# A scan as four plus three accumulating matmuls a batch: four consecutive rows on a partition, and the steps of neighbouring batches interleaved

## What is computed

```python
def _L0_xattn_ref(q, k, v):
    kv = jnp.swapaxes(k * v, 0, 1)
    def step(r, kv_t):
        r = DECAY * r + kv_t          # DECAY = 0.9
        return (r, r)
    _, rs = jax.lax.scan(step, r0, kv)
    return q * jnp.swapaxes(rs, 0, 1)
...
x = x + _L0_xattn_ref(_layernorm(x), ctx, ctx)
x = x + _L0_ffn_ref(_layernorm(x), w1, b1, w2, b2)
```

## Time and profile before

| | |
|---|---|
| median of 3 runs | 1266.23 us (1264.81 to 1266.30) |
| the profiled execution's own time | 1265.31 us |
| its span, first to last instruction | 1263.5 us |
| scan stage, by the chain that ended last | 0 to 315.9 us |
| scales and first quantization | 315.9 to 329.2 us |
| first product (second stage) | 329.2 to 800.5 us |
| second product (third stage) | 807 to 1263.5 us |
| busy: PE, ACT, DVE, POOL | 96%, 78%, 69%, 13% of the span |
| mean granted clock of PE | 0.987 of full |

### The profile page before, as it was taken

How to read it: one execution, slowest core, us unless ns; L and a number is a source line. 1 busy time by engine, 2 the same in 40 slices (tenths; PEclk the granted TensorE clock), 3 DMA queues, 4 the chain that set the end, 5 groups by cost and what they waited for, 6 DMA issues and landing times.

```text
span 1263.5 us, 15533 instructions
## 1 busy us (share of the span) xinstructions
PE 1213.5 (96%) x5386; PEld 562.1 (44%) x5386; DVE 872.2 (69%) x1262; ACT 979.9 (78%) x1211; POOL 162.3 (13%) x394
## 2 busy tenths in 40 slices
PE   5998999999699999999999999799999999999997
PEld 2444444444344444444444444344444444444443
DVE  4887999886577777777777777566545655654554
ACT  4788999887577777777777776688887888888776
POOL 2646556444000000000000000000000000000000
PEclk9999999999799999999999999899999999999999
DMA  9999999972277799999999998699999999999998
GB/s 354 403 406 333 389 363 341 346 277 81 118 321 289 305 394 407 359 365 362 362 358 351 348 363 317 229 334 419 418 417 417 417 418 417 417 418 416 416 417 325
DMA packets 134614, 448.78 MB, mean 355 GB/s; under 512 B 10740, under 2 KB 10760, under 8 KB 123400
## 3 DMA queue, kind: packets, MB, share of 16 engines
q1 hardware_dynamic: 94744, 331.40, 66.2%
q10 hardware_dynamic: 39792, 116.40, 25.8%
HBM read 254.81 MB, written 192.94 MB: 354 GB/s over the span
## 4 chain that ended last, share of the span: by engine, by line
PE 80%; POOL 6%; issue 5%; DVE 4%; DMA 3%; ACT 2%; SPq 1%; ACTq 0%; POOLq 0%; DVEq 0%
PE ps L833 35%; PE ps L875 33%; PE ps L811 9%; PE ps L855 2%; DMA xq<-hidden_scratch 2%; POOL xq L444 2%; DVE st L644 1%; DVE st L630 1%; DVE xq L639 1%; DMA xq<-in_x_dram 1%; POOL rstd L436 1%; POOL cs_bc L428 1%; ACT xq L478 1%; ACT xq L589 0%; SPq L317 0%
## 5 line engine op out<-in xcount | busy, mean ns | idle before, releaser
L875 PE MATMUL ps<-w2T,xq 128*128 128x512 f16 x2048 | 446.4, 381 | 4.2 <-ACT xq L589 3.8
L833 PE MATMUL ps<-xq,w1T 128*128 128x512 f16 x2048 | 448.7, 380 | 1.4 <-DVE xq L710 1.4
L589 ACT ACTIVATE xq<-xq,hb,hs 128x512 f16<-128x512 f32 x494 | 357.3, 801 | 83.6 <-PE ps L875 57.5
L701 DVE TENSOR_REDUCE work<-xq 128x2 f32<-128x1024 f32 x255 | 311.0, 1220 | 125.9 <-ACT xq L534 125.9
L534 ACT ACTIVATE xq<-ps 128x1024 f32<-128x1024 f32 x255 | 260.9, 1023 | 123.1 <-PE ps L833 122.9
L875 PEld LDWEIGHTS ps<-w2T,xq 128*128 128x128 f16 x2048 | 200.0, 98 | 250.6 <-ACT xq L589 9.8
L811 PE MATMUL ps<-xq,work 128*128 128x512 f32 x640 | 283.0, 603 | 24.7 <-ACT xq L468 24.7
L833 PEld LDWEIGHTS ps<-xq,w1T 128*128 128x128 f16 x2048 | 199.1, 98 | 237.0 <-issue 1.9
L749 DVE TENSOR_TENSOR work<-ps,cs_bc 128x512 f32<-128x512 f32 x128 | 88.4, 691 | 185.0 <-PE ps L875 178.6
L811 PEld LDWEIGHTS ps<-xq,work 128*128 128x128 f32 x640 | 122.9, 193 | 178.0 <-issue 161.0
L478 ACT ACTIVATE xq<-ps,ones,cs_bc 128x512 f32<-128x512 f32 x128 | 98.9, 772 | 24.8 <-PE ps L811 23.8
(11 more groups left out here) (99 smaller groups left out, 444.9 us busy)
## 6 DMA issues: line engine op xcount, KB each, us to landing
hidden_scratch<-xq SPq DMA_DIRECT2D x240, 512.0 KB, 6.0
xq<-hidden_scratch SPq DMA_DIRECT2D x232, 512.0 KB, 21.2
work<-x_scratch ACTq DMA_DIRECT2D x42, 1024.0 KB, 11.4
xq<-in_ctx_dram ACTq DMA_DIRECT2D x31, 1024.0 KB, 9.2
xq<-in_x_dram SPq DMA_DIRECT2D x24, 1024.0 KB, 12.0
x_scratch<-xq SPq DMA_DIRECT2D x24, 1024.0 KB, 8.4
out_dram<-work ACTq DMA_DIRECT2D x24, 1024.0 KB, 12.0
xq<-in_L_ffn_w_dram SPq DMA_DIRECT2D x8, 1024.0 KB, 7.8
```

The costliest lines, as they stand in the source:

```text
L589: act.activation(hq[c % HQ], src[:, c % 2, :], ACT.Relu, bias=hb[:, q:q + 1], scale=hs[:, q:q + 1]).then_inc(h_scaled, 1)
L701: dve.tensor_reduce(hmax[:, b * NF + 2 * q:b * NF + 2 * q + 2], src, AX.X, ALU.max).then_inc(kept_maxed, 1)
L833: last = pe.matmul(bank, w1T[:, k, f * P:(f + 1) * P], xq_rows(b, k), start=(k == 0), stop=(k == KD - 1))
L875: last = pe.matmul(acc_bank(s, i), src[:, i * P:(i + 1) * P], w2T[:, q, :], start=first, stop=final)
```

## The change

**Four consecutive rows a partition.** Row `4 p + i` of a batch now lies on partition `p` as tile `i`, for x, ctx and the output; a partition's part of a transfer is one piece of 8 KB.

**Seven matmuls.** With that order the scan over a batch is a scan over partitions of the sum of a partition's four rows (each weighted), and then a step from row to row within the partition. A batch has one bank. `scan_first(j, k)` for `k` = 0..3 sums four products into it, and what stands there is tile 0. `scan_next(j, i)` for `i` = 1..3 adds one product with a scaled identity (`own_mat`) to the same bank, and what stands there is tile `i` up to a factor that is put into the constants of the statistics (`half_x`, `per_row_x`, `eps_x`). ACT has to have read tile `i - 1` from the bank before `scan_next(j, i)` may write: a wait of PE for ACT (`scan_scaled`) in each of the three steps, and ACT waits for PE (`scan_ready`) for the next one.

**Interleaving.** To have work between these steps, PE's list puts the four of batch j+2 between the single steps of batches j and j+1. Tiles are worked off in the order (j+1, 0), (j, 2), (j+1, 1), (j, 3), written out in `tiles`, and `scans` is the order in which banks come ready. ACT, DVE and the stores of SP count by these lists.

**Around it.** `ctx` has four buffers and not three, x is loaded six batches ahead and not five, x's statistics are taken four batches ahead and not three (`XLEAD`), the statistics rings hold eight batches and not four, `g1` has four tiles in turn and not two batches, POOL's list has the statistics of both kinds in odd batches and the rounding in even ones, and the square of batch j+3 stands at the end of ACT's batch j, before the steps for the weights. The load of the first weight quarter stands after five x batches and not after three. POOL and DVE make some more constants at the start. The second and third stage are unchanged but for the output's row order.

```diff
-    x_rows = x.rearrange("b (i p) d -> b p i d", p=P)
-    ctx_rows = ctx_in.rearrange("b (i p) d -> b p i d", p=P)
-    out_rows = out.rearrange("b (i p) d -> b p i d", p=P)
+    x_rows = x.rearrange("b (p i) d -> b p i d", p=P)
+    ctx_rows = ctx_in.rearrange("b (p i) d -> b p i d", p=P)
+    out_rows = out.rearrange("b (p i) d -> b p i d", p=P)
...
-CS = 3
-RING = 4
-LEAD = 5
+CS = 4
+RING = 8
+XLEAD = 4
+LEAD = 6
...
+    scans, tiles = [(0, 0)], []
+    for j in range(-1, NB):
+        scans += [t for t in ((j + 1, 1), (j, 3), (j + 1, 2), (j + 2, 0)) if 0 <= t[0] < NB]
+        tiles += [t for t in ((j + 1, 0), (j, 2), (j + 1, 1), (j, 3)) if 0 <= t[0] < NB]
+    scan_at = {t: n for n, t in enumerate(scans)}
+    tile_at = {t: n for n, t in enumerate(tiles)}
...
             def load_ctx(j):
-                wait_count(act, scan_ready, (j - CS + 1) * NI)
+                if j >= CS:
+                    act.wait_ge(scan_ready, scan_at[(j - CS, NI - 1)] + 1)
...
-                act.wait_ge(scan_ready, u + 1)
-                wait_count(act, x2_done, u + 1 - 2 * NI)
-                act.activation(g1[j % 2][:, i, :], scan_bank(j, i), ACT.Identity, bias=ones[:, 0:1],
+                act.wait_ge(scan_ready, scan_at[(j, i)] + 1)
+                wait_count(act, x2_done, n + 1 - len(g1))
+                act.activation(g1[n % len(g1)], scan_bank(j), ACT.Identity, bias=ones[:, 0:1],
...
             square(0)
+            factors(0, 0)
+            square(1)
+            factors(0, 1)
+            square(2)
             for j in range(NB):
-                factors(j, 0)
-                factors(j, 1)
                 if j + 1 < NB:
-                    square(j + 1)
+                    factors(j + 1, 0)
                 factors(j, 2)
-                factors(j, 3)
+                if j + 1 < NB:
+                    factors(j + 1, 1)
                 if j + CS < NB:
                     load_ctx(j + CS)
+                factors(j, 3)
+                if j + 3 < NB:
+                    square(j + 3)
                 for m in weights_at(j - 1):
                     int_weights(m)
                 for m in weights_at(j - 3):
...
+            for n in range(2, NU):
+                j, i = divmod(n - 2, NI)
+                product(n)
+                y_stats(n - 1)
+                if j < NB - 1:
+                    x_stats(j + XLEAD, i)
+                if i == NI - 1:
+                    for m in weights_at(j):
+                        weight_scales(m)
...
-            def scan(j, i):
-                u = j * NI + i
-                wait_count(pe, scan_scaled, u - 5)
-                kv, bank = ct[j % CS], scan_bank(j, i)
-                terms = [(k, kv[:, i - k, :]) for k in range(i + 1)]
-                for k, rows in terms:
-                    last = pe.matmul(bank, decay_mat[:, k * P:(k + 1) * P], rows, start=(k == 0), stop=(k == terms[-1][0]))
-                last.then_inc(scan_ready, 1)
+            def scan_first(j, k):
+                if not 0 <= j < NB:
+                    return
+                if k == 0:
+                    pe.wait_ge(ctx_squared, j + 1)
+                    if j >= 6:
+                        pe.wait_ge(scan_scaled, tile_at[(j - 6, NI - 1)] + 1)
+                last = pe.matmul(scan_bank(j), decay_mat[:, k * P:(k + 1) * P], ct[j % CS][:, k, :], start=(k == 0), stop=(k == NI - 1))
+                if k == NI - 1:
+                    last.then_inc(scan_ready, 1)
+
+            def scan_next(j, i):
+                if not 0 <= j < NB:
+                    return
+                pe.wait_ge(scan_scaled, tile_at[(j, i - 1)] + 1)
+                pe.matmul(scan_bank(j), own_mat[:, (i - 1) * P:i * P], ct[j % CS][:, i, :], start=False, stop=True, skip_group_check=True).then_inc(scan_ready, 1)
...
-            for j in range(NB):
-                pe.wait_ge(ctx_squared, j + 1)
-                for i in range(NI):
-                    scan(j, i)
+            for j in range(-1, NB):
+                scan_first(j + 2, 0)
+                scan_next(j + 1, 1)
+                scan_first(j + 2, 1)
+                scan_next(j, 3)
+                scan_first(j + 2, 2)
+                scan_next(j + 1, 2)
+                scan_first(j + 2, 3)
                 for m in weights_at(j - 2):
                     turn_weights(m)
```

More of the change, by code:

```diff
@@ L387, in _ @@
             gp.memset(ones[:, :], 1.0)
-            gp.memset(decays, DECAY)
+            gp.memset(decays, DECAY ** NI)
+            for i in range(NI):
+                gp.memset(half_x.rearrange("p (n i) -> p n i", i=NI)[:, :, i], 0.5 * DECAY ** -i)
+                gp.memset(per_row_x.rearrange("p (n i) -> p n i", i=NI)[:, :, i], DECAY ** (-2 * i) / D)
+                gp.memset(eps_x.rearrange("p (n i) -> p n i", i=NI)[:, :, i], LN_EPS * DECAY ** (-2 * i))
             gp.memset(neg_half[:, :], -0.5)
@@ L393, in _ @@
             gp.wait_ge(gp_step, 1)
-            for m, w in ((impulse, 4 * P), (ident[:, :], P), (ident_b[:, :], P)):
+            for i in range(NI):
+                part = impulse[:, i * P:(i + 1) * P]
+                gp.affine_select(out=part, in_=part, compare_op=ALU.not_equal, fill=DECAY ** (NI - i) if i else 1.0, base=1 if i else 0,
+                                 pattern=[[-1, P]], channel_multiplier=1)
+            for i in range(1, NI):
+                gp.memset(decays[:, i * P:i * P + 1], 0.0)
+            for m in (ident[:, :], ident_b[:, :]):
                 last = gp.affine_select(out=m, in_=m, compare_op=ALU.not_equal, fill=1.0, base=0,
-                                        pattern=[[-1, w]], channel_multiplier=1)
+                                        pattern=[[-1, P]], channel_multiplier=1)
             last.then_inc(consts_ready, 1)
@@ L405, in step, with row_stats @@
                 gp.wait_ge(gp_step, stepped[0])
-            def row_stats(pw, st, mean, factor):
+            def row_stats(pw, st, mean, factor, per, halves, floor):
                 n = st.shape[1]
@@ L415, in row_stats @@
                 gp.tensor_tensor(mean, t[0], factor[:, 0:n], ALU.mult)
[L416 to L418 removed]
+                gp.tensor_tensor(t[3], t[1], per[:, 0:n], ALU.mult)
+                step(gp.tensor_tensor(t[4], t[2], halves[:, 0:n], ALU.mult))
+                gp.tensor_tensor(t[5], t[3], floor[:, 0:n], ALU.add)
                 step(gp.tensor_tensor(t[6], t[4], t[4], ALU.mult))
@@ L448, in _ @@
             x_stats(x_group[1])
-            for j in range(NB):
-                if j % 2 == 1 and j + 1 < NB:
-                    x_stats(x_group[j + 1])
-                if j % 2 == 0 and j >= 2:
-                    y_stats(y_group[j - 1])
+            x_stats(x_group[2])
+            for j in range(NB - 2):
+                if j % 2 == 1:
+                    if j + XLEAD < NB:
+                        x_stats(x_group[j + XLEAD])
+                    y_stats(y_group[j])
                 for m in weights_at(j):
@@ L611, in _ @@
             link(dve.tensor_tensor_scan(decay_mat, decays, impulse, 0.0, ALU.mult, ALU.add))
+            for i in range(1, NI):
+                link(dve.tensor_scalar(own_mat[:, (i - 1) * P:i * P], ident[:, :], DECAY ** -i, None, ALU.mult))
             def weight_scales(m):
```

68 lines of the change are left out of this document (37 added, 31 removed).

## The result

The changed kernel took 1271.88 us (median of 8 runs, 1270.03 to 1275.49), the kernel before beside it 1265.05 us (8 runs, 1264.57 to 1266.40). The ratio is 1.0056, 95% interval 1.0043 to 1.0069. The forecast of 1251 us was wrong, in sign and in range. The profiled execution took 1270.98 us, its span is 1269.2 us, mean granted clock 0.969 (0.987 before).

What follows compares the result with a forecast made beforehand. The scan stage's end was taken to carry the kernel's end, PE alone bounding the last 13 batches. Last bank read 304.4 us for 315.9, -11.5, and third stage -2 gave -13.5: 1251 us, range 1225 to 1266.

Steps and rivals of the forecast that it cites:

- the third stage: Output stores in longer pieces need less DMA time, so late PE and ACT waits go: -2 us (bounds 0 and -6).
- the handshake: Scan stage: ACT and PE wait for each other over the later tiles, about 0.55 us a batch, bounds 0 and 1.2.
- the count of falls: Scan stage: the clock falls seven times, once in each later pair of batches with weights.
- start, to square(3): Scan stage's start, both lists walked through from ACT's first centring at 18.6 us: square(3) at 35.5 us.
- seven pairs with weights: Scan stage: pairs of batches with weight quarters, each 20.5 us including a fall of the clock, 143.5 us together.
- last copies, iterations 18 to 27: Scan stage: last weight copies 1.8 us, then ten iterations without weights at 7.6 us, 76 us.
- The clock: Scan stage: PE idles some 4.2 us behind weight steps, seven times; the clock then falls and the bank comes 1.85 us later.
- Transfers: 8 KB pieces run at 417 GB/s, not 387: a batch's DMA floor is 7.5 us instead of 8.1.
- the second regime: Scan batches without weights, PE alone bounding at 8.6 us; only there are the saved matmuls (2.6 us a batch) on the path.
- The fifth: Rival, slower: the clock falls in iterations without weights too, twelve falls at 1.8 us, 1273 us; chance 0.10.
- The second (no fall): Rival: the clock stays up in the scan stage's pairs with weights, 12.5 us less, 1239 us; chance 0.23.
- The third (engines at their floors): Rival: handshake, transfers and POOL are not felt, ACT's own work bounds the scan stage, 1219 us; chance 0.12.

Runs made afterwards that it cites:

- e6: Kernel before with only the new row order for x, ctx and output (scan then runs over wrongly ordered rows): 1266.92 us, ratio 1.0012.
- e5: Changed kernel with only the output's transfers back in 2 KB pieces (output rows in another order): 1268.71 us, ratio 1.0032 to the kernel before.
- e12: As e11, but each output store cut into two transfers of every second tile, 2 KB pieces, row order kept: 1239.64 us.
- e10: Changed kernel with three useless matmuls more a batch, so ten again in the new order: 1305.11 us, ratio 1.0311 to the kernel before.
- e2: Changed kernel plus two or four useless matmuls in each of nine PE gaps behind ACT's weight steps: 1254.45 us, ratio 0.9915 to the kernel before.
- e11: As e4, plus one useless matmul in each of two PE gaps in iterations with weights: 1242.88 us, ratio 0.9828 to the kernel before.
- e3: Changed kernel with ACT's weight steps spread one by one between the tiles of the next iterations: 1247.55 us, ratio 0.9868 to the kernel before.
- e4: Changed kernel with weight steps spread between tiles and the ctx load behind the fourth tile's bank read: 1238.84 us, ratio 0.9802.
- e9: Changed kernel with weight steps spread, ctx load between fourth tile's centring and read, two useless matmuls in iterations with weights: 1237.86 us.
- e1: Changed kernel with ACT's ctx load moved behind the fourth tile's bank read: 1263.52 us, ratio 0.9986 to the kernel before.
- e7: Changed kernel with ACT's ctx load moved between the fourth tile's centring and its bank read: 1265.11 us, ratio 0.9994 to the kernel before.

## Why the prediction was wrong, step by step

The sum had 304.4 us for the last bank read's end; it is 316.7, 12.3 us more. The total was to be -13.5 us and the span grew by 5.7. No single step carries that; nearly all erred to one side. The steps that failed are the third stage (-2 us, where it lost 3.4), the handshake (0.55 us a batch, where it took 0.86) and the count of falls (seven, where nine came).

| step | predicted | measured | off |
|---|---|---|---|
| start, to square(3) | 35.5 | 37.7 | +2.2 |
| iteration 1 and first pair | 25.6 | 25.6 | 0.0 |
| seven pairs with weights | 143.5 | 147.9 | +4.4 |
| last copies, iterations 18 to 27 | 77.8 | 83.9 | +6.1 |
| end of the stage | 22 | 21.5 | -0.5 |
| last read to first product | 0 (to 1) | +1.0 | +1.0 |
| second stage | 0 | +0.4 | +0.4 |
| third stage | -2 | +3.4 | +5.4 |

**The start.** ACT's first centring began at 19.20 and not at 18.6 us, ACT stood 0.90 us for PE before the read at 30.41, and 0.76 us before the centring at 34.50, the handshake's price below: together the 2.2 us.

**The clock: right in kind.** All seven idle times that I named (3.87 us; I had 4.2) were followed by a fall, on average at the predicted price: 21.13 a pair, the mean of 20.7 to 22.1, is 2 x 7.78 + 3.72 + 1.85. The Trainium skill ("TensorE: Matmul & The Clock Gate", Part 1) has the throttled state as the default, by which all seven fall; the trace of the changed kernel agrees, nine of nine from 1.98 us on. **The count failed**: the fall belongs to the iteration behind the weight step, so the seventh of 3.87 us falls behind the last pair, and the last copies alone (1.98 us idle) give another. Both landed in what I had called iterations without weights: some 4.3 of the 6.1 us.

**The handshake was mis-sized.** I took 0.55 us with bounds 0 and 1.2; it is 0.86. I had counted the wait for the bank (0.49) and forgotten that the queue's issue behind it takes ACT 0.38 us more, time which was free only as long as ACT had nothing late. With 7.78 for 7.6 it gives 1.8 us in the ten iterations, and it is what makes the pairs 0.6 us longer than forecast.

**Transfers.** The start's loads, mostly 8 KB pieces, do run faster than the 387 GB/s of 2 KB pieces (DMA, 12 to 25 us, changed kernel; e6, where only the row order differs, has 413 GB/s there):

```profile
DMA packets 805, 5.45 MB, mean 419 GB/s; under 512 B 108, under 2 KB 108, under 8 KB 150
```

The Trainium skill ("DMA: Bandwidth & Descriptors", Specifications) has 512 B as enough for line rate; where loads are alone, 387 against 419 GB/s speaks against that. **In the third stage my step failed**: there the mix ran at 417 GB/s before and at 416 with longer pieces, so nothing was to be had, as the Trainium skill has it. What the pieces changed: the stores landed in 8.0 for 12.5 us, ACT stood longer for the loads of the sums, and PE waited 4.3 for 1.8 us (e5, e6; e12 by its time). That the stores took their share of the rate from these loads is only argued. In the 420 us from the second product's start the loads' queue moved 112.3 MB in the changed kernel and 113.2 in e5, which fits, but 113.5 in e6 and 113.4 before, and the median load of the sums landed no later (20.8 for 21.5 us, 850 to 1200 us).

**What was right:** PE's saving is off the path for the most part (I took 1.0 of the 2.6 us a batch in the second regime; e10 gives 1.29 less 0.47, 0.82). 13 batches times 0.82 are 10.7 us, and that is the whole gain. It was spent in the pairs, 20.0 us before (82.65 to 202.79, six pairs) and 21.1 now, and in the two falls behind them.

**The rivals.** The fifth, slower, gave 1273 us and was closest, but by another mechanism: it wanted falls in the iterations without weights, and there the clock was 1.00. Its price of 1.8 us a fall was right; two of its twelve came, behind the weights. The second (no fall) is e2: 1254 us, not 1239, since the handshake and the third stage's loss stand. The third (engines at their floors) is what e11 reaches in its later pairs (17.54 us for 2 x 6.9 + 3.7).

## What to carry to other kernels

Before you thin out an engine's work, look where its idle time will lie: nine gaps of 2.0 to 3.9 us cost 16 us in clock (e2), more than the 10.7 us that the batches without weights gained, and spreading another engine's long steps between its short ones (e3) turned a loss of 0.6% into a gain of 1.3%, 2.0% with one load moved (e4). In a chain where two engines hand each other tiles, count every instruction in the waiting engine's list, a queue's issue too, and move what isn't needed there behind the next hand-over. Where transfers already run at the rate of the mix, longer pieces need not help: here they made the stores land earlier at the same rate, and the kernel some 3 us slower (e5, e12). Ask which queue the bound engine waits for.

## What the runs showed of the hardware beyond that

- The length of an idle time doesn't alone decide on the clock. In the changed kernel 1.98 and 2.04 us were followed by a fall; in the kernel before 2.61 us was not once; in e4 2.58 us (at 115.54) was not, 2.92 us (at 133.98) was; in e10 3.01 us was not (at 185.93), and was in the six other places.
- Useless matmuls can pay: e2 is 17.4 us faster for them, though they are up to four more matmuls in every second iteration of the stretch with weights, and e9 8.2 us. They need not: e11 is 4 us slower than e4.
- The stores' piece length, 8 KB for 2 KB, changes their landing from 12.5 to 8.0 us at an unchanged total rate of 416 to 417 GB/s.
- The kernels with the ctx load moved alone (e1, e7) spread over 14.5 and 10.9 us from run to run, others over 2 to 6. In both the fastest execution has the highest mean clock (0.968, 0.969) and the slowest the lowest (0.957, 0.958). That the late ctx does it is not shown: e4 and e11 wait for ctx for 10.5 and 9.8 us and spread over 6 and 1.7.
